# Second and third attention: maxima first in each step, value products of a key tile in every second step, outputs turned in the banks of the maxima

## The reference, cut to what matters

```python
q, k, v = (proj(w_q), proj(w_k), proj(w_v))        # (B, heads, S, 16)
scores = jnp.einsum('bhqd,bhkd->bhqk', q, k) / jnp.sqrt(jnp.float32(16))
attn = jax.nn.softmax(scores, axis=-1)
out = jnp.einsum('bhqk,bhkd->bhqd', attn, v)
```

## Time and profile before

| | us |
|---|---|
| median of 3 runs (lowest, highest) | 2761.74 (2758.88, 2776.99) |
| the profiled execution | 2762.35 |
| its span | 2760.6 |
| stretch of the exponentials, `l1a` | 1194.2 to 1590.8 |
| stretch of the exponentials, `l2a` | 1852.0 to 2243.2 |

### The profile page before, as it was taken

One profiled execution on the slowest core, in us unless ns is written; L12 is line 12 of the kernel. 1 busy time (PEld: TensorE's weight loads), 2 busy tenths in 40 slices (PEclk: granted clock), 3 DMA queues, 4 the chain that ended last, 5 costly groups with the idle time before them and its releaser, 6 DMA issues. The chain is left out here.

```text
span 2760.6 us, 29801 instructions
## 1 busy us (share of the span) xinstructions
PE 2230.8 (81%) x10640; PEld 1250.1 (45%) x10640; DVE 1399.9 (51%) x1933; ACT 1264.6 (46%) x2097; POOL 630.0 (23%) x460
## 2 busy tenths in 40 slices
PE   4989999999997977478888757478888786998757
PEld 3657777777776733232222223222222233443434
DVE  3564545555552445577888163177888513103153
ACT  3545556556563222046777732017777742001321
POOL 1645655656552023200000022100000001001021
PEclk8989999999998988568999878789999988999878
DMA  4861111111112102302110002511121003000001
GB/s 106 245 206 39 46 57 54 42 57 54 43 42 89 61 22 90 77 1 36 18 26 10 1 16 91 129 17 24 30 41 24 1 16 123 0 0 0 18 12 47
DMA packets 78930, 138.70 MB, mean 50 GB/s; under 512 B 30808, under 2 KB 40792, under 8 KB 78832
## 3 DMA queue, kind: packets, MB, share of 16 engines
q1 hardware_dynamic: 78832, 137.40, 18.2%
HBM read 95.95 MB, written 41.03 MB: 50 GB/s over the span
## 5 line engine op out<-in xcount | busy, mean ns | idle before, releaser
L2139 POOL TENSOR_TENSOR l0a_p_low<-yT,l0a_p_high 128x1024 fp32r<-128x1024 f32 (+7 forms) x256 | 386.0, 1536 | 282.3 <-ACT l0a_p_high L2167 282.3
L173 POOL TENSOR_TENSOR applied<-prepared,neghalf 128x2 f32<-128x2 f32 x64 | 58.4, 913 | 1546.0 <-DVE prepared L154 1546.0
L1421 DVE TENSOR_REDUCE l2a_mx<-ps 128x2 f32<-128x1024 f32 x256 | 307.8, 1224 | 114.3 <-PE ps L1305 113.4
L1421 DVE TENSOR_REDUCE l1a_mx<-ps 128x2 f32<-128x1024 f32 x256 | 308.5, 1224 | 98.2 <-PE ps L1305 97.3
L1402 ACT ACTIVATE l1a_prob<-ps 128x512 f32<-128x512 f32 x512 | 278.0, 595 | 112.9 <-PE ps L1332 74.2
L1402 ACT ACTIVATE l2a_prob<-ps 128x512 f32<-128x512 f32 x512 | 278.0, 595 | 106.6 <-PE ps L1332 69.5
L2200 DVE TENSOR_REDUCE l0a_mx<-ps 128x1 f32<-128x512 f32 (+3 forms) x384 | 203.6, 553 | 236.2 <-PE ps L2046 145.3
L2156 ACT ACTIVATE yT<-ps 128x1024 f32<-128x1024 f32 (+7 forms) x256 | 166.3, 650 | 187.2 <-PE ps L2068 123.5
L1332 PE MATMUL ps<-l1a_q,l1a_k 49*128 49x512 f32 x512 | 135.0, 524 | 68.5 <-ACT l1a_prob L1402 64.4
L1332 PE MATMUL ps<-l2a_q,l2a_k 49*128 49x512 f32 x512 | 133.3, 518 | 69.1 <-ACT l2a_prob L1402 64.3
L2167 ACT CAST l0a_p_high<-yT 128x1024 fp32r<-128x1024 f32 (+7 forms) x256 | 172.6, 674 | 7.1
(11 more groups left out here) (297 smaller groups left out, 4233.4 us busy)
## 6 DMA issues: line engine op xcount, KB each, us to landing
l0a_q<-l0a_q SPq DMA_DIRECT2D x32, 512.0 KB, 3.3
l0q_woh<-in_l0a_wo SPq DMA_DIRECT2D x16, 512.0 KB, 5.2
l0a_q<-f SPq DMA_DIRECT2D x32, 256.0 KB, 4.6
l0a_q<-l0q_q_pe SPq DMA_DIRECT2D x32, 256.0 KB, 3.6
l0a_recip_rows<-l0a_recip_row SPq DMA_DIRECT2D x32, 256.0 KB, 3.4
l0a_o<-l0a_o_pair SPq DMA_DIRECT2D x16, 512.0 KB, 2.8
yT<-l0a_o SPq DMA_DIRECT2D x16, 512.0 KB, 3.3
l1a_q<-l1a_q_parts SPq DMA_DIRECT2D x16, 256.0 KB, 5.5
```

What stands on the lines that cost most here:

```text
L1421: nc.vector.tensor_reduce(mx[:, g % 2, :, p, qt, c], banks(("pair", m)), AX.X, ALU.max).then_inc(s_red, 1)
L2139: nc.gpsimd.tensor_tensor(p_low[:, j % 4, P * j:T], prob[:, j % 4, P * j:T], p_high[:, j % 4, P * j:T], ALU.subtract).then_inc(s_pl, 1)
```

## The change

Value products of key tiles 0 to 6 are issued at steps 5, 7, ..., 17, that of key tile 7 at step 18, and each is cut into two column halves of 256 queries, issued one behind the other. In a TensorE step the maxima, the turning of maxima and the turning of outputs now come ahead of the wait for the exponential, and scores and value products behind it. The turned outputs go to a bank pair of the maxima's ring rather than back to `O`; so the first value product waits for ScalarE's copy only, the turning waits for a ring bank, and a later pair of maxima waits for the multiplication. ScalarE copies `O` between the two exponentials of step 19 rather than behind both; the turning moves from step 20 to step 21.

```diff
-PV_STEP = (7, 8, 9, 10, 12, 14, 16, 18)
-OUT_STEP, TURN_OUT_STEP, FINISH_STEP = 19, 20, 21
+PV_STEP = [(2 * j + 5, 2 * j + 5) for j in range(7)] + [(18, 18)]
+OUT_STEP, TURN_OUT_STEP = 19, 21
...
-    rden = sb("rden", [P, NT // 2, GROUP])
+    rden = sb("rden", [P, 2, NT // 2, GROUP])
...
+        if at >= TURN_OUT_STEP and (at - TURN_OUT_STEP) % (2 * NT) == 0:
+            ring.append(("out", (at - TURN_OUT_STEP) // (2 * NT)))
+    ring.append(("out", GROUPS * HALVES - 1))
...
+        elif kind == "out":
+            engine.wait_ge(s_out, b_out + n + 1)
...
-            def pv(g, half, j):
-                if j == 0 and (g or half):
-                    pe.wait_ge(s_out, b_out + HALVES * g + half)
+            def pv(g, half, j, c):
+                if j == 0 and c == 0 and (g or half):
+                    pe.wait_ge(s_oev, b_oev + HALVES * g + half)
...
                 pe.wait_ge(s_exp, b_exp + 2 * ((HALVES * g + half) * 2 * NT + 2 * j + 2))
+                cut = slice(256 * c, 256 * c + 256)
                 for hh in range(GROUP):
-                    mm = nc.tensor.matmul(O[32 * hh:32 * hh + 32, :], vext[:, j, g * GROUP + hh if OWN_KEYS else g, :],
-                                          prob[:, j % 4, hh, :], start=j == 0, stop=j == NT - 1)
-                mm.then_inc(s_pv, 1)
+                    mm = nc.tensor.matmul(O[32 * hh:32 * hh + 32, cut], vext[:, j, g * GROUP + hh if OWN_KEYS else g, :],
+                                          prob[:, j % 4, hh, cut], start=j == 0 and c == 0,
+                                          stop=j == NT - 1 and c == 1)
+                if c == 1:
+                    mm.then_inc(s_pv, 1)
...
                 pe.wait_ge(s_oev, b_oev + n + 1)
+                wait_bank(pe, ("out", n))
                 for t in range(NT // 2):
-                    mm = nc.tensor.transpose(O[:, t * P:(t + 1) * P], osb[:, t * P:(t + 1) * P], chip.ident[:])
+                    mm = nc.tensor.transpose(banks(("out", n))[:, 0, t * P:(t + 1) * P], osb[:, t * P:(t + 1) * P], chip.ident[:])
...
             for at in range(TOTAL):
+                for m in max_at.get(at, []):
+                    max_pair(m)
+                if turn_at.get(at // STEPS + 1) == at and at % STEPS == TURN_STEP:
+                    max_turn(at // STEPS + 1)
+                n = half_ended(at, TURN_OUT_STEP)
+                if n is not None:
+                    o_turn(n)
                 pe.wait_ge(s_exp, b_exp + 2 * at + 1)
                 if at + 1 < TOTAL:
                     scores(at + 1)
-                for m in max_at.get(at, []):
-                    max_pair(m)
-                n = half_ended(at, TURN_OUT_STEP)
-                if n is not None:
-                    o_turn(n)
                 for job in pv_at.get(at, []):
                     pv(*job)
-                if turn_at.get(at // STEPS + 1) == at and at % STEPS == TURN_STEP:
-                    max_turn(at // STEPS + 1)
...
                 for hf in range(2):
                     nc.scalar.activation(prob[:, j % 4, 2 * p + hf, :], st(at, hf), ACT.Exp,
                                          scale=SCALE).then_inc(s_exp, 1)
-                n = half_ended(at, OUT_STEP)
-                if n is not None:
-                    o_out(n)
+                    n = half_ended(at, OUT_STEP)
+                    if hf == 0 and n is not None:
+                        o_out(n)
```

More of the change, by code:

```diff
@@ L1246, in attend @@
             for j in range(NT):
-                pv_at.setdefault(min((HALVES * g + half) * 2 * NT + PV_STEP[j], TOTAL - 1), []).append((g, half, j))
+                for c in range(2):
+                    at = (HALVES * g + half) * 2 * NT + PV_STEP[j][c]
+                    pv_at.setdefault(min(at, TOTAL - 1), []).append((g, half, j, c))
     def half_ended(at, lag):
@@ L1334, in scores @@
                 mm.then_inc(s_st, 1)
-            def pv(g, half, j):
-                if j == 0 and (g or half):
-                    pe.wait_ge(s_out, b_out + HALVES * g + half)
-                if j == 0 and not (g or half):
+            def pv(g, half, j, c):
+                if j == 0 and c == 0 and (g or half):
+                    pe.wait_ge(s_oev, b_oev + HALVES * g + half)
+                if j == 0 and c == 0 and not (g or half):
                     pe.wait_ge(s_vout, b_vout + NT)
                 pe.wait_ge(s_exp, b_exp + 2 * ((HALVES * g + half) * 2 * NT + 2 * j + 2))
+                cut = slice(256 * c, 256 * c + 256)
                 for hh in range(GROUP):
-                    mm = nc.tensor.matmul(O[32 * hh:32 * hh + 32, :], vext[:, j, g * GROUP + hh if OWN_KEYS else g, :],
-                                          prob[:, j % 4, hh, :], start=j == 0, stop=j == NT - 1)
-                mm.then_inc(s_pv, 1)
+                    mm = nc.tensor.matmul(O[32 * hh:32 * hh + 32, cut], vext[:, j, g * GROUP + hh if OWN_KEYS else g, :],
[3 more added lines that the diff above has]
+                    mm.then_inc(s_pv, 1)
             def o_turn(n):
                 pe.wait_ge(s_oev, b_oev + n + 1)
+                wait_bank(pe, ("out", n))
                 for t in range(NT // 2):
-                    mm = nc.tensor.transpose(O[:, t * P:(t + 1) * P], osb[:, t * P:(t + 1) * P], chip.ident[:])
+                    mm = nc.tensor.transpose(banks(("out", n))[:, 0, t * P:(t + 1) * P], osb[:, t * P:(t + 1) * P], chip.ident[:])
                 mm.then_inc(s_ot, 1)
@@ L1429, in finish @@
                 dve.wait_ge(s_ot, b_ot + n + 1)
-                both = O.rearrange("p (t h e) -> p t h e", h=GROUP, e=2 * HD)
-                nc.vector.reciprocal(rden[:], both[:, :, :, HD]).then_inc(s_rd, 1)
+                both = banks(("out", n))[:, 0, :].rearrange("p (t h e) -> p t h e", h=GROUP, e=2 * HD)
+                nc.vector.reciprocal(rden[:, n % 2], both[:, :, :, HD]).then_inc(s_rd, 1)
                 dve.wait_ge(s_rd, b_rd + n + 1)
@@ L1434, in finish @@
                 nc.vector.tensor_tensor(rows.rearrange("p t (h e) -> p t h e", e=HD), both[:, :, :, 0:HD],
-                                        rden[:].unsqueeze(3).broadcast_to([P, NT // 2, GROUP, HD]),
+                                        rden[:, n % 2].unsqueeze(3).broadcast_to([P, NT // 2, GROUP, HD]),
                                         ALU.mult).then_inc(s_out, 1)
@@ L1444, in _ @@
                     reduce_pair(m)
-                n = half_ended(at, FINISH_STEP)
+                n = half_ended(at, TURN_OUT_STEP)
                 if n is not None:
```

## The result

The changed kernel takes 2801.07 us (median of 4 runs, 2791.17 to 2806.86) against 2769.36 for the kernel before beside it (4 runs, 2758.88 to 2779.78): ratio 1.0111, 95% interval [1.0055, 1.0166]. Ratios leave out runs more than 1.5% above the fastest of their kernel, so one can differ from the quotient of the medians.

A forecast was written before the change was run, and what follows sets the result against it. No engine is full; a chain between engines sets the pace. Terms -27.2 + 13.6 + 7.8 + 14.3 + 5.0 + 1.5 = +15.0, with -12 for the clock, gave 2765 us from 2762.35; range 2738 to 2798.

The forecast's parts named there:

- The clock: Half-clock falls in the sparse stretch at a half's start: half of 23.8 us won back, -12; bounds -24 and +25.
- Rival 3: Added waits in the sparse stretch make the clock fall more often: 2802 us, or 2777 if nothing is gained; chance 0.12.
- The steady rhythm: Steady steps: issuing maxima first gains nothing, as the order is a circle; 0, bounds 0 and +0.09 a value product.
- the signs given, 1.19 and 1.7: Expected gaps in us between scores of successive steady steps: 1.19 without value products, 1.7 with them.
- The cut: Value products in two pieces: two more changes of pass, 0.053 us a key tile, +13.6 in all.
- Rival 1: Weight loads show in each pass of the cut value products: +0.2 a key tile, 2803 us; chance 0.15 with the swap.
- The first value product: Moved to step 5, it no longer delays the fifth key tile's exponential: 0.85 us saved a half, -27.2.
- The copy: Between step 19's exponentials, it waits for the value product and delays the next scores: 0.26 us more a half, +7.8.
- The turning behind the reduction: At step 21 the turning waits for VectorE's reduction of step 20's maxima: gap 1.80 us, +0.55 a half, +14.3.
- The turning of maxima: Next maxima, step 11 of the second half, wait for banks VectorE is reducing: +0.42 us in six groups, two layers, +5.0.
- Half to half at full clock: Expected sign: the time from one half to the next at full clock is 24.1 and 24.7 us.
- The ends: In a layer's last half, key tile 5's value product moves past one more exponential: about 0.75 us a layer, +1.5.

The follow-up runs named there:

- experiment 2: Unread matmul pairs added in the steps without maxima: to the changed kernel, 2757.18 us, ratio 0.9995; to the kernel before, 2752.38 us, ratio 0.9971.
- experiment 3: Changed kernel with old steps in last group, 2793.15 us; with no cut, 2783.16; with both in last group, 2785.74; kernel before with the cut, 2768.42.
- experiment 4: Changed kernel with column halves in two steps, 2694.42 us; plus unread matmul pairs, 2677.92; also with output turning and copy moved, 2658.98.

## Why the prediction was wrong

- **The clock** is the step that failed. The term was -12, with bounds -24 and +25. It looked at the sparse stretch at a half's start alone, took that stretch as shorter, and priced an added fall at what one cost before, 3.9 us: it had no term for a fall that lasts.
- **What the runs showed in its place.** In the profile the clock's part came out at about +35, outside both bounds (an estimate: 44.5, less 3.6 outside the layers and 6 of full-clock cost). In the last groups there weren't more falls but fewer; they lasted, 58 to 75 us in all six last groups profiled of the changed kernel, where before they were over in 10.2 and 6.8. That is +27.4 where -6 or so was taken. Another part came in the first halves of the second layer, which have maxima, with one fall of 34 and one of 27 us; in the other two profiles the second layer has no such falls. Before, four value products stood in a row (steps 7 to 10) ahead of the clock's return; after, nearly each is followed by a step with two matmuls of scores only, and is cut in two. Filling the same steps took the clock's loss in the last groups back (experiment 2), so the sparse steps without maxima are shown as the cause there; which property of them makes a fall last is shown in part only (experiment 3).
- **The number.** The range (2738 to 2798) missed 2801.07 by 3, and ten further runs of the changed kernel had a median of 2790.46, inside it; that would have been luck, as the clock term was wrong in each of the three profiles. Rival 3 had the price (2802) by luck too: six more falls of 3.9 in halves with maxima, where there were long ones, mostly without.
- **The steady rhythm** was right: 1.77 and 1.09 are 2.86 for 2.85; the scores land 0.1 sooner after maxima, as estimated, and the value-product gap is 0.1 longer for it, so the signs given, 1.19 and 1.7, were 0.10 and 0.07 off, one each way. Splitting over two steps shows the other side of the same argument (experiment 4).
- **The cut** was mis-sized: 0.053 a key tile was taken, 13.6 in all. The value product takes 1.00 (1422.79 to 1423.79) as it did before, and halves with and without the cut differ by 0.03 at most (experiment 3), so it costs under 0.01 a key tile, 2 us at most. Its four passes start 0.24, 0.22 and 0.22 apart, where 256 columns streamed twice are 0.21: only the first change of pass costs 0.03. Rival 1 is out: its +0.2 would have made the value product 1.2.
- **The first value product**: -0.85 a half, right; the gap that took 2.51 is 1.77, as any with value products.
- **The copy** costs 0.16 more a half (gap 1.43 for 1.27) where 0.26 was taken; the mechanism is as told. The copy starts 1.46 after the scores of its step (1417.44 in the trace to 1418.90) for 1.60: the value product stands 0.32 behind them, not 0.42, and isn't longer for the cut. Its wait is 0.43; the sign given, about 0.6, didn't fit the prediction's own terms (1.60 - 0.54 - 0.60 = 0.46).
- **The turning behind the reduction**: gap 1.84 for 1.80 forecast, TensorE idle 0.54 for VectorE. Right.
- **The turning of maxima**: the gap behind it is 1.52 for 1.61; with its neighbours (2.07 and 1.67, for 1.88 and 1.66, of which the swap's 0.1 goes back) +0.43 for +0.42. Right.
- **Half to half at full clock** came out at 23.85 and 24.48: 26 halves with maxima cost 6 us more than before. The forecast's own terms give 24.2 and 24.9 (the signs said 24.1 and 24.7) and +15 for these halves, and the difference is the cut. With the last group's clock evened out, the two kernels stand 5 apart (experiment 2).
- **The ends** (+1.5) can't be read: both layers of the profile after end at half clock.

## What to carry to other kernels

When a change moves TensorE's work about, look at the sparsest stretch it runs through, not at the typical one, and ask two things of the clock there: whether it falls, and how long a fall lasts. Here the second was missed: falls of 10.2 and 6.8 us became falls to the layer's end, and that cost more than the waits one counts. The same rhythm was seen at both clocks, so one profile doesn't settle what a rhythm does; filling the sparse steps did. In a loop of engines write the order down as a circle: moving an operation across a wait changed nothing here (2.86 for 2.85), as the same pieces stood between the same two links; cutting a piece changed nothing either while both parts stayed in one step; dividing it over two steps did (2.46).

## What the runs showed of the hardware that was not expected

- Two matmuls of 512 columns a step that nobody reads, in 80 steps of two layers, kept the granted clock of the last groups at 1.00 in place of 0.50 to 0.58 and made the changed kernel faster, by 33 us by the medians (2790.46 to 2757.18) and 14 by the ratios.
- In the last groups of the changed kernel the clock's loss repeated from one execution to the next to 0.1 us a layer (60.4 or 64.8 us), while between the layers it came in two forms, 64.7 us at 0.92 and 81.4 us at 0.71, for the same instructions.
- The same steps ran at either clock: 21.4 us at 1.00 and 31.6 us at 0.50, one half behind the other in one layer (experiment 3).
- An fp32 value product of 512 columns cut in two takes 1.00 us as the whole one does, four column strips side by side, its passes 0.24, 0.22 and 0.22 apart.
